# A four-stage graph network on one core: GpSimd zeros 256 columns of an idle buffer behind every fourth gather

## The reference, cut to what matters

```python
def _gcn_layer(x, W, b, src, dst, norm, n_nodes):      # layer 0, twice
    xt = x @ W
    msg = xt[src] * norm[:, None]
    agg = jax.ops.segment_sum(msg, dst, num_segments=n_nodes)
    return jax.nn.relu(agg + b)
...
h = jnp.concatenate([x[row], x[col]], axis=-1)         # layer 2
msgs = jax.nn.silu(h @ W1.T + b1) @ W2.T + b2
agg = jax.ops.segment_sum(msgs, row, num_segments=n_nodes)
...
mf = (x @ W_f.T)[row] * ew[:, None]                    # layer 3, forward and backward
y_forward = jax.ops.segment_sum(mf, col, num_segments=n_nodes)
mb = (x @ W_b.T)[col] * ew[:, None]
y_backward = jax.ops.segment_sum(mb, row, num_segments=n_nodes)
```

## Time and profile before

| | |
|---|---|
| time before, median of 3 | 7039.76 us (7037.64 to 7044.29) |
| profiled execution, its own time | 7040.77 us |
| its span, first to last instruction | 7039.0 us |
| share of the span that PE, PE's weight load, DVE, ACT, POOL were busy | 76%, 54%, 59%, 32%, 61% |
| gathers in the five passes | 888 + 4 x 880 = 4408 |
| TensorE's mean granted clock, share of full speed | 0.75 |

### The profile page before, as it was taken

How to read it: one execution, slowest core, us unless ns; L and a number is a source line. 1 busy time by engine, 2 the same in 40 slices (tenths; PEclk the granted TensorE clock), 3 DMA queues, 4 the chain that set the end, 5 groups by cost and what they waited for, 6 DMA issues and landing times. The chain is left out here.

```text
span 7039.0 us, 121911 instructions
## 1 busy us (share of the span) xinstructions
PE 5336.7 (76%) x24856; PEld 3780.6 (54%) x24857; DVE 4129.6 (59%) x9445; ACT 2274.6 (32%) x3599; POOL 4297.0 (61%) x4461
## 2 busy tenths in 40 slices
PE   5567777789999998998888887996666665666664
PEld 4456666657777765775555554553443443444442
DVE  8977777547777776987777775663232222332224
ACT  3322222238888862023333332441111111111111
POOL 1367777737777772006777773006777777777774
PEclk8567777689999999579999998995555555555555
DMA  3144444443333330333333334112221113222212
GB/s 98 37 117 132 129 132 130 133 132 103 104 103 103 103 104 16 120 133 107 105 105 105 105 105 103 31 30 64 65 65 53 53 53 50 53 53 53 53 53 71
DMA packets 309259, 608.63 MB, mean 86 GB/s; under 512 B 89530, under 2 KB 163590, under 8 KB 309064
## 3 DMA queue, kind: packets, MB, share of 16 engines
q0 software_dynamic: 184128, 466.71, 24.8%
q1 hardware_dynamic: 125064, 141.13, 6.5%
HBM read 563.79 MB, written 50.13 MB: 87 GB/s over the span
## 5 line engine op out<-in xcount | busy, mean ns | idle before, releaser
L893 PE MATMUL banks<-ring,oh 128*128 128x128 f32 x3520 | 1381.6, 498 | 834.2 <-DMA ring<-fwd_table,stage_i 421.1
L893 PEld LDWEIGHTS banks<-ring,oh 128*128 128x128 f32 x3520 | 879.9, 311 | 1336.0 <-issue 1335.6
L1285 ACT ACTIVATE banks<-iota 128x1024 f32<-128x1024 f32 x442 | 454.0, 1027 | 2573.2 <-DVE acc L1938 1918.4
L637 POOL DMA_INDIRECT ring<-h_table,stage_i x880 | 852.3, 969 | 356.0 <-PE banks L970 191.4
L637 POOL DMA_INDIRECT ring<-fwd_table,stage_i x880 | 830.2, 943 | 332.6 <-PE banks L893 184.3
L637 POOL DMA_INDIRECT ring<-bwd_table,stage_i x880 | 830.2, 943 | 273.9 <-PE banks L893 229.2
L1312 ACT ACTIVATE ring<-big 128x889 f16<-128x889 f16 x840 | 874.0, 1041 | 198.3 <-PE banks L981 165.1
L981 PE MATMUL banks<-ring,big 128*128 128x445 f16 (+1 forms) x3360 | 774.6, 352 | 0.0
L667 POOL DMA_INDIRECT big<-x_and_degree,stage_i x536 | 521.5, 973 | 202.0 <-issue 112.7
L1919 DVE TENSOR_TENSOR oh<-banks,s_loc 128x512 f32<-128x512 f32 x220 | 152.1, 692 | 804.7 <-PE banks L893 804.6
L1919 DVE TENSOR_TENSOR oh<-banks,d_loc 128x512 f32<-128x512 f32 x220 | 152.1, 692 | 780.0 <-PE banks L893 779.9
(11 more groups left out here) (445 smaller groups left out, 8608.9 us busy)
## 6 DMA issues: line engine op xcount, KB each, us to landing
big<-places_in_block SPq DMA_DIRECT2D x111, 256.0 KB, 3.5
acc<-places_in_block SPq DMA_DIRECT2D x74, 384.0 KB, 3.4
ring<-h_table,stage_i POOLq DMA_INDIRECT x880, 2.7
ring<-fwd_table,stage_i POOLq DMA_INDIRECT x880, 2.5
ring<-bwd_table,stage_i POOLq DMA_INDIRECT x880, 2.5
big<-x_and_degree,stage_i POOLq DMA_INDIRECT x536, 2.9
h_table<-hq SPq DMA_DIRECT2D x50, 128.0 KB, 1.7
x_table<-ring SPq DMA_DIRECT2D x25, 256.0 KB, 2.1
```

The costliest lines, as they stand in the source:

```text
L637: pool.indirect_dma_start(out=gbuf[:, u % RING, 0:width], out_offset=None, in_=table, in_offset=bass.IndirectOffsetOnAxis(ap=stage_i[:, v, ...
L893: pe.matmul(sums_by(h, P)[:, ds(slot, 1), :].rearrange("p a f -> p (a f)"), oh[:, u, :], gbuf[:, u, 0:P], start=False, stop=False, skip_gr ...
L1285: act.activation(sums_by(h, P), iota[:, :].unsqueeze(1).to_broadcast([P, 1024 // P, P]), ACT.Copy, scale=0.0).then_inc(S["sums_cleared"], 1)
```

## The change

Behind every fourth gather GpSimd writes zeros into the first 256 columns of `tile_oh`, through the view `spacer`. That is done in all five passes, except for the first forty gathers of pass 1: 848 of its 888 gathers give 212 such memsets, and each other pass gives 220, together 1092. Nobody reads what they write. Each memset waits on the semaphore `spaced` until the one before it is complete, and adds one to it; a first count is given ahead. Since the number of semaphores is limited, `spaced` takes the place of `sp_waited`, a counter that no one waits on, and SyncE steps `act_waited` in its place, on which no one waits either.

```diff
+        SPACED = 4
+        spacer = tile_oh[:, :, :].rearrange("p g b -> p (g b)")[:, 0:D]
...
-                apart(sp, S["sp_waited"])
+                apart(sp, S["act_waited"])
...
+            pool.sem_inc(S["spaced"], 1)
+
+            def space(n):
+
+                pool.wait_ge(S["spaced"], n + 1)
+                apart(pool, S["pool_waited"])
+                pool.memset(spacer, 0.0).then_inc(S["spaced"], 1)
+
+            writes_before = lambda k: (T - LONG) // SPACED + TILES // SPACED * (k - 1)
+
             def gathers(k, table, width, free, base):
...
                                                 in_offset=bass.IndirectOffsetOnAxis(ap=stage_i[:, v, u % RING:u % RING + 1], axis=0)).then_inc(gd[u % RING], 16)
+                        if (u + 1) % SPACED == 0:
+                            space(i * (SPAN // SPACED) + u // SPACED + writes_before(k))
...
                                             in_offset=bass.IndirectOffsetOnAxis(ap=stage_i[:, v, r:r + 1], axis=0)).then_inc(landed, 16)
+                    if not first and (u + 1) % SPACED == 0:
+                        space((i - 1) * (LONG // SPACED) + u // SPACED)
...
                                             in_offset=bass.IndirectOffsetOnAxis(ap=stage_i[:, v, u % RING:u % RING + 1], axis=0)).then_inc(gd[u // GROUP], 16)
+                    if (u + 1) % SPACED == 0:
+                        space(i * (SPAN // SPACED) + u // SPACED + writes_before(2))
```

More of the change, by code:

```diff
@@ L335, in build @@
         gate_done spa_in spa_out pass_ready p_split l2_oh l2_t l2_cp l2_p l2_add l2_silu
-        l2_c l2_acc sqrt_in sqrt_out x2_done x2_mul x2_stat x2_agg x2_std x2_inv x2_out sp_waited p_diff p_high p_mid g_agg g_t1 g_a1 g_ab g_rz g_n
+        l2_c l2_acc sqrt_in sqrt_out x2_done x2_mul x2_stat x2_agg x2_std x2_inv x2_out spaced p_diff p_high p_mid g_agg g_t1 g_a1 g_ab g_rz g_n
         g_tanh g_xn g_ms1 g_std1 g_ms2 g_std2 g_done gru_in x2t_in x2t_out x3_done x_bias f_out f_bias y_sum y_stat y_agg y_std y_inv y_out w5_in y_ready""".split()
```

## The result

The changed kernel takes 7243.36 us in the median (7243.13 to 7247.06), against 7042.02 us (7037.64 to 7046.38) for the kernel before beside it. The ratio is 1.0287, 95% interval 1.0274 to 1.0300: 201.3 us more, 0.184 us for each of the 1092 memsets. The forecast was 7265 us, 225 us more, in a range of 7075 to 7425. The direction and the mechanism (time added to GpSimd's queue is added to the kernel) were right, and the added time came 24 us too high, from two errors of opposite sign: 25 us too little in the net of a memset, over 40 us too much for contention with VectorE.

A forecast was written before the change was run, and what follows sets the result against it. The prediction took GpSimd's queue to bound all five passes. It added 47 us (pass 1), 64 (pass 2), 42 (pass 3) and 72 (passes 4 and 5), together 225 us, giving 7265 us, range 7075 to 7425.

The forecast's parts named there:

- The bound: All five passes, some 5600 of 7039 us: GpSimd's queue sets their end, with about 0.305 us idle between gathers.
- The wait and the steps at nothing: Each memset's wait and counter step: no cost, covered by queued gathers; without cover some 0.1 us each.
- The memset's 0.308 us: Length of a 256-column memset on GpSimd: 201 ns for 128 columns plus 128 x 0.834 ns, 308 ns.
- Nothing ahead of it and 0.16 us behind: Idle time on GpSimd beside each memset: 0 before it and 0.16 us before the next gather.
- The check by the first pair of the earlier trace: Gathers with a 0.20 us cast between start 1.31 us apart, not 1.25; scaled to a memset, this gives 0.17 us.
- The net, 0.163 us: Time each memset adds to GpSimd's queue in every pass: 0.308 + 0.16 - 0.305 = 0.163 us.
- Contention, 47 us of the sum: Memsets held by VectorE instructions: 0.06 us each in pass 1, 0.126 in pass 2, 0.03 in pass 3, 0 later.
- Hidden in the gap: Rival, 0.15: the memset fits into the 0.305 us between gathers, leaving only some 45 us of contention; 7085 us.
- Added in full: Rival, 0.15: the 0.305 us belongs to a gather's start, so each memset adds its whole 0.308 us; 7421 us.
- Held by VectorE: Rival, 0.05: each of 652 memsets in passes 1 to 3 loses 0.76 us to VectorE; 7714 us.
- The clock of pass 3: Rival, 0.03: longer gaps bring PE's clock to 0.5 for all of pass 3, 720 us more; 7990 us.
- Faster: Rival, 0.07: a memset takes 0.247 us in place of the 0.305 between gathers; 6977 us, or 7020 with contention.

The follow-up runs named there:

- p45: The changed kernel with its 256-column memsets in passes 4 and 5 alone, 440 of them; 7122.43 us against 7041.09 for the kernel before, ratio 1.0116.
- half45: The kernel before, with the gathers of passes 4 and 5 fetching only the first 64 of each tile's 128 rows; 6949.52 us, ratio 0.9871.
- w8_s4: The changed kernel with memsets of 8 columns in place of 256; 7052.98 us against 7045.82 for the kernel before, ratio 1.0009.
- dep_later: The changed kernel, the second gather behind a memset waiting for it; 8503.3 us against 8481.8 for the kernel before, again 8441.5 against 8411.9.
- dep256: The changed kernel, the gather right behind each memset waiting for it; 8256.15 us against 7045.82 for the kernel before, ratio 1.1718.
- copy8_s4: The changed kernel with a GpSimd copy of 8 columns in place of each memset; 7128.26 us against 7045.82 for the kernel before, ratio 1.0117.

## Why the prediction was right, point by point

**The bound: right.** It was read from five passes with one rate and a constant idle time; the wait of 87.1 us ahead of pass 2 that the sum for that pass takes off isn't in rows 3, but the trace's waits have it (L637, longest 87.1). The nearly equal 41 to 42 us of the five passes show it, and for passes 4 and 5 p45 and half45 as well.

**The wait and the steps at nothing: right.** w8_s4 has all 1092 of them and costs at most 7 ns each. That queued gathers are the cover is what dep_later shows for a wait one gather away. The price named for a lost cover, some 0.1 us, was wrong by a factor of nine: dep256 measured 0.92, and the 0.84 us behind the first cast of the kernel before could have told. A forecast that had rested on it would have missed by hundreds of us.

**The memset's 0.308 us: somewhat low.** It was worked out from memsets in the preparation. Between gathers a memset is recorded some 0.02 us longer: 0.123 us for 8 columns against 0.104 in the preparation, and 0.330 for 256 against the 0.308 worked out. The slope, 0.834 ns a column, held.

**Nothing ahead of it and 0.16 us behind: right,** 0 and 0.165. I had called the 0.16 rather much, since the gather behind the cast waits for its result. That was misread: it waits for an earlier one, so rows 6 are the same case as a memset's. The check by the first pair of the earlier trace rows, 1.31 us from start to start, was therefore a sound one, and copy8_s4 gives 1.309 to 1.311 us in every pass. Scaled by the 0.13 us by which a memset between gathers is longer than that cast's 0.20, in place of 0.11, it gives 0.19.

**The net, 0.163 us: mis-sized by 0.02.** Measured: 0.186 by the starts. Times 1092 that is 203 us, against the 178 of the forecast's term.

**Contention, 47 us of the sum: this step failed.** It measured some 4 us, what all memsets last beyond their median: the per-memset price is nearly the same in all passes, and copy8_s4 costs no more in passes 1 to 3. I had priced every VectorE instruction that a memset meets at half of its length (0.19 us for an `oh` of pass 2), while the 130 memsets that met one last 7 ns more than the median, and those that meet one with two SBUF inputs nothing (w8_s4). The gathers' median of 946 ns spoke against it, which I used only against the rival. VectorE paid instead, 385 to 425 ns for `oh` in pass 2, and that is hidden as forecast. So 178 + 47 became 203 + 4 or less, and that the total came within 24 us is in part luck: the error of one term hid over half of that of the other.

**The rivals.** *Hidden in the gap* falls for 256 columns but holds for 8: which case applies is a matter of length. *Added in full* falls with the 0.165 us. *Held by VectorE* falls: pass 2's longest memset was 0.376 us, and of pass 1's only thirteen lasted over 0.4. *The clock of pass 3* falls, too. These are stretches of passes 2 and 3 of the changed kernel, answering to the earlier trace rows: PE, PEld, DVE, ACT, POOL busy, then clock, DMA share and GB/s.

```profile
1900.00:2300.00 400.00, 391.36 (x1829) 269.98 (x1828) 298.97 (x723) 320.07 (x343) 317.99 (x381) 1.00 0.35 100
3800.00:4400.00 600.00, 490.07 (x2756) 331.66 (x2754) 426.05 (x1150) 215.37 (x402) 475.41 (x579) 1.00 0.36 100
```

PE's share in pass 3 fell from 0.845 to 0.817, as foreseen, and the granted clock stayed at 1.00, which is its 2.4 GHz level. *Faster* was the one with a wrong condition: less than 0.305 us together. w8_s4 had 0.288 by its sum and gained nothing, since the gap is a floor. By that rule no length of the memset makes this kernel faster.

The Trainium skill's rule (Perfetto Trace Analysis, section "GPSIMD Engine Instruction"), timing by the distance of starts, gave 7197 us where the recorded duration gave 7265; 7243 was measured. Between gathers the recorded length and the idle time behind it describe the change to 4 ns (0.190 against 0.186), so here the trace doesn't bear out the discount taken from memsets that follow each other at once. The distance of the gathers' own starts, 0.186, does agree with the time measured (1092 x 0.186 = 203 us against 201).

## What to carry to other kernels

A constant idle time between like instructions, the same in passes with different work, means that their engine sets the rate, even at a busy share of 0.75. Some of that time can be used: here a GpSimd instruction behind a gather is all but free up to 0.305 - 0.165 = 0.14 us (an estimate: a memset of about 28 columns, by 0.123 us at 8 and 0.83 ns a column; 8 and 64 were run), costs what it lasts beyond that, and gained nothing in any run where GpSimd sets the rate. A wait ahead of an indirect DMA costs nothing while another gather is queued between it and the instruction that it waits for, and 0.92 us without one; look for such a pair in the trace before pricing it.

## What the runs showed of the hardware that I had not expected

- Half of the rows make issuing a gather 5% shorter (0.897 against 0.944 us for 64 and 128 rows); by these two points most of it doesn't depend on the rows.
- The 0.305 us between two gathers runs on beside another instruction of GpSimd, but is never cut short by it.
- A gather that waits for the memset right ahead of it starts 0.90 us after it at the least, 1.06 in the mean (dep256); behind the first cast of the kernel before it is 0.84.
- A GpSimd copy of 8 columns that begins beside a VectorE instruction with two SBUF inputs lasts up to 0.949 us instead of 0.196; 74 memsets of 8 columns beside such instructions lasted 0.132 at most.
- With a memset behind every gather, each gather is recorded 7 ns longer (951 against 944 ns), nearly all that 8 columns cost.
- In two of the four sets of runs the kernel before took 8482 and 8412 us instead of 7042, and two chips had both: 7041 us on chip 12 in one set and 8482 in another, 7046 and 8412 on chip 8. There a memset behind every gather came out 0.5% and 1.6% faster than the kernel before, and in the kernels traced there pass 3 ran with a granted clock of 0.80 to 0.85 instead of 1.00. The cause is open.
